# The first mixture's combine: row normalisation by ScalarE with a scale and a bias from GpSimd, in place of VectorE

## The reference, cut to what matters

```python
def _layernorm(x, axis=-1, eps=1e-05):
    m = jnp.mean(x, axis=axis, keepdims=True)
    v = jnp.var(x, axis=axis, keepdims=True)
    return (x - m) / jnp.sqrt(v + eps)

# end of layer 1: two experts for each row, weighted, and one shared expert
x = _layernorm(x + moe(x))            # moe: combine(expert_out) + 0.1 * shared
# start of layer 2
qkv = x @ W_qkv + b_qkv               # 16 heads of 8, alibi bias, softmax, values
```

## Time and profile before

| what | value |
|---|---|
| time, three runs | 1142.61, 1149.12, 1151.37 us; median 1149.12 |
| the profiled execution | 1147.93 us, span 1146.2 us |
| mean granted clock of TensorE | 0.925 |
| TensorE busy (matmuls) | 987.9 us, 86% |
| VectorE busy | 780.8 us, 68% |
| ScalarE busy | 660.6 us, 58% |
| GpSimd busy | 352.7 us, 31% |

### The profile page before, as it was taken

How to read it: one execution, slowest core, us unless ns; L and a number is a source line. 1 busy time by engine, 2 the same in 40 slices (tenths; PEclk the granted TensorE clock), 3 DMA queues, 4 the chain that set the end, 5 groups by cost and what they waited for, 6 DMA issues and landing times.

```text
span 1146.2 us, 18859 instructions
## 1 busy us (share of the span) xinstructions
PE 987.9 (86%) x6456; PEld 500.3 (44%) x6517; DVE 780.8 (68%) x1663; ACT 660.6 (58%) x1282; POOL 352.7 (31%) x541
## 2 busy tenths in 40 slices
PE   5599889999988799366999999898899998988992
PEld 2267634544445588332333333476322222224661
DVE  5976686768742411489788887246888888855875
ACT  4664646566554355052667767575277766685451
POOL 7636510111442335420000000231111221645764
PEclk9799879999999899766999999989599999899997
DMA  5930224333621220333333210002234432311332
GB/s 142 171 73 1 93 102 140 129 119 106 174 79 31 65 64 17 89 94 107 100 122 123 80 65 31 2 1 93 99 112 146 132 99 77 110 29 46 98 102 84
DMA packets 98375, 101.70 MB, mean 89 GB/s; under 512 B 13354, under 2 KB 80571, under 8 KB 98199
## 3 DMA queue, kind: packets, MB, share of 16 engines
q1 hardware_dynamic: 86169, 89.28, 26.6%
q0 software_dynamic: 6432, 8.18, 2.5%
q10 hardware_dynamic: 5680, 3.04, 1.0%
HBM read 66.60 MB, written 38.09 MB: 91 GB/s over the span
## 4 chain that ended last, share of the span: by engine, by line
PE 66%; DVE 18%; issue 5%; ACT 5%; POOL 4%; DMA 2%; SPq 0%; another core or an unknown queue 0%; ACTq 0%; POOLq 0%; DVEq 0%
PE PS L894 13%; PE PS L878 13%; PE PS L851 8%; DVE negm L1696 5%; PE PS L705 5%; PE PS L700 5%; PE PS L1063 3%; PE PS L1073 3%; PE PS L1193 3%; PE PS L881 3%; PE PS L854 2%; PE PS L902 2%; ACT arena L1323 2%; PE PS L1208 2%; DVE X L1551 1%
## 5 line engine op out<-in xcount | busy, mean ns | idle before, releaser
L1323 ACT ACTIVATE arena<-PS 128x512 f32<-128x512 f32 (+3 forms) x768 | 362.5, 548 | 187.9 <-PE PS L881 121.1
L1696 DVE TENSOR_REDUCE negm<-PS 128x2 f32<-128x1024 f32 (+3 forms) x384 | 404.7, 1087 | 89.2 <-PE PS L851 44.5
L878 PE MATMUL PS<-arena 128*128 128x512 bf16 (+3 forms) x707 | 219.8, 363 | 8.4 <-ACT arena L1323 5.1
L894 PE MATMUL PS<-arena,VPAD 128*32 128x512 f32 (+3 forms) x1536 | 188.1, 561 | 0.1
L851 PE MATMUL PS<-arena 32*128 32x512 bf16 (+3 forms) x768 | 144.3, 374 | 29.5 <-DVE negm L1696 25.9
L851 PEld LDWEIGHTS PS<-arena 32*128 32x128 bf16 x768 | 36.4, 91 | 213.4 <-DVE negm L1696 106.9
L878 PEld LDWEIGHTS PS<-arena 128*128 128x128 bf16 x768 | 69.7, 98 | 120.3 <-issue 57.1
L2533 POOL CAST nmp<-negm 128x16 bf16<-128x16 f32 x48 | 9.4, 196 | 360.7 <-DVE negm L1696 241.1
L700 PE MATMUL PS<-arena,W 128*128 128x512 f32 x144 | 84.1, 719 | 12.4 <-ACT arena L1241 9.9
L705 PEld LDWEIGHTS PS<-W,arena 128*128 128x128 f32 x640 | 80.0, 204 | 14.0 <-issue 7.1
L705 PE MATMUL PS<-W,arena 128*128 128x128 f32 x640 | 81.6, 288 | 3.0 <-DVE arena L1640 2.7
(11 more groups left out here) (335 smaller groups left out, 1538.1 us busy)
## 6 DMA issues: line engine op xcount, KB each, us to landing
arena<-score_q SPq DMA_DIRECT2D x48, 288.0 KB
arena<-score_k SPq DMA_DIRECT2D x48, 288.0 KB
arena<-max_parts SPq DMA_DIRECT2D x48, 256.0 KB
max_parts<-arena SPq DMA_DIRECT2D x36, 256.0 KB, 2.9
score_k<-arena SPq DMA_DIRECT2D x36, 128.0 KB
score_q<-arena SPq DMA_DIRECT2D x12, 384.0 KB
arena<-rows_y SPq DMA_DIRECT2D x16, 256.0 KB, 3.9
arena<-slots SPq DMA_DIRECT2D x46, 65.0 KB, 1.9
```

The source lines that it names most:

```text
L878: mm = pe.matmul(PS[:, b, q0:S], OK[s][:, r, kt * P:(kt + 1) * P], OQ[s][:, r, q0:S], start=True, stop=True)
L894: mm = pe.matmul(PS[32 * r:32 * r + 32, 7, q0:S], VP[:, u, kt, r, :], PB[:, kt % 2, r, q0:S], start=(kt == 0), stop=True, skip_group_check ...
L1323: act.activation(PB[:, kt % 2, r, q0:S], PS[:, 4 + use % 3, q0:S], ACT.Exp, scale=slope(u % G, r) if o["slope"] else 1.0).then_inc(exped, 1)
L1696: vec.tensor_reduce(negm[:, u % 2, 2 * rp:2 * rp + 2, qt], PS[:, 2 * (use % 2):2 * (use % 2) + 2, 0:nk], AX.X, ALU.max, negate=True).then_ ...
```

## The change

The step `ln` leaves VectorE and becomes a step of ScalarE: four `activation` instructions with function Identity, the scale `rs` and the bias `nb` = -mean * rs. GpSimd computes `nb` in two further instructions behind the power. TensorE's transposes wait for ScalarE in place of VectorE. The orders of ScalarE and VectorE are rewritten; those of TensorE and GpSimd stay. ScalarE now goes ln 0, xT 0, q 0, k 0 (with the zeros), ln 1, ln 3, xT 1, q 1, k 1 (with the zeros), xT 3, q 3, k 3, ln 2, xT 2, q 2, k 2. VectorE goes tot 0, tot 1, tot 3, split 0, tot 2, split 1, values 0, values 1, and from there on as before. What is computed stays the same.

```diff
-    "cb.a cb.tot", NORM_V.format("cb"), PREP_V.format("p2"),
+    "cb.a cb.tot cb.bn cb.mv", PREP_V.format("p2"),
...
-    "p1.xT p1.q p1.k o1.xT r1.xT", numbered("sh.h", 4), EXPERTS_A, "p2.xT p2.q p2.k",
+    "p1.xT p1.q p1.k o1.xT r1.xT", numbered("sh.h", 4), EXPERTS_A, "cb.ln p2.xT p2.q p2.k",
...
-COMBINE_SCALAR, COMBINE_SCALAR_TURNS = words("xT q k"), "000111333222"
-COMBINE_VECTOR, COMBINE_VECTOR_TURNS = words("tot ln split values"), "001103321201RR3RRRRRRRR32RRR2R"
+COMBINE_SCALAR, COMBINE_SCALAR_TURNS = words("ln xT q k"), "0000131113332222"
+COMBINE_VECTOR, COMBINE_VECTOR_TURNS = words("tot split values"), "01302101RR3RRRRRRRR32RRR2R"
...
                     if step == "tr":
-                        turned_input(c, "p2", "cb.ln")
+                        pe.wait_ge(*A.at(c, "cb.ln"))
+                        turn(c, lanes[c].A, lanes[c].X, "p2.tr")
...
                 for step, c in taken(COMBINE_SCALAR, COMBINE_SCALAR_TURNS):
-                    if step == "xT":
+                    if step == "ln":
+                        L = lanes[c]
+                        act.wait_ge(*PO.at(c, "cb.nb"))
+                        act.wait_ge(*V.at(c, "cb.tot"))
+                        for j in range(CT):
+                            t = act.activation(L.X[:, j, :], L.tot[:, j, :], ACT.Identity, scale=L.rs[:, j:j + 1], bias=L.nb[:, j:j + 1])
+                        t.then_inc(*A.did(c, "cb.ln"))
+                    elif step == "xT":
...
-                    elif step == "ln":
-                        normalised(c, L.tot, L.X, "cb")
...
+                    L = lanes[c]
                     norm(c, "cb")
+                    pool.tensor_scalar(L.nb[:], L.mv[:, :, 0], -1.0, 0.0, ALU.mult, ALU.add).then_inc(*PO.did(c, "cb.nm"))
+                    pool.wait_ge(*PO.at(c, "cb.nm"))
+                    pool.tensor_tensor(L.nb[:], L.nb[:], L.rs[:], ALU.mult).then_inc(*PO.did(c, "cb.nb"))
```

More of the change, by code:

```diff
@@ L115 @@
     "m.va m.rs m.va2 m.rs2 m.lva m.lrs t.va t.rt t.rs t.s2 t.s1 t.va2 t.rt2 t.rs2 t.lva t.lrs o1.lva o1.lrs",
-    "x0.id x1.id cb.lva cb.lrs o2.xb o2.lva o2.lrs ch.xb ch.lva ch.lrs o3.xb r3.id r3.lva r3.lrs r3.nm r3.nb o3.lva o3.lrs r3.sh e.lva e.lrs"]))
+    "x0.id x1.id cb.lva cb.lrs cb.nm cb.nb o2.xb o2.lva o2.lrs ch.xb ch.lva ch.lrs o3.xb r3.id r3.lva r3.lrs r3.nm r3.nb o3.lva o3.lrs r3.sh e.lva e.lrs"]))
 TENSOR_STEPS = words(" ".join([
```

## The result

The changed kernel takes 1152.62 us, the median of 20 runs (1147.48 to 1157.07), against 1146.24 for the kernel before in 20 runs (1142.02 to 1151.99). The ratio is 1.0049 with a 95% interval of 1.0034 to 1.0065, so the change costs 3.9 to 7.5 us, 5.6 by the ratio. The forecast was 7.5 us more than before and 1156.0 us in all; both kernels lie within the 1% of each other that the prediction expected. The profiled execution took 1155.99 us with a span of 1154.0, against 1147.93 and 1146.2.

A forecast was written before the change was run, and what follows sets the result against it. VectorE's chain and ScalarE's with TensorE arrive together at the first maxima; after the change the latter is later. The sum 1.0 + 0.5 + 3.1 + 2.8 + 0.1 = 7.5 us more gave 1156.0 us, range 1150 to 1162.

The forecast's parts named there:

- Step 1: Chunk 0 ahead of its transposes: two added GpSimd instructions and the slower norm on ScalarE, together +1.0 us.
- Step 2: Chunk 0's roots on GpSimd: held up by VectorE's two-input instructions of tot 1, +0.5 us, between 0 and 1.3.
- Step 3: Chunk 1's copy on ScalarE: ln 1 and ln 3 now stand ahead of it, +3.1 us, 4.6 late in all.
- Step 4: Chunk 2: ln 2 queued behind k 3 on ScalarE makes its transposes 7.4 us late, 2.8 beyond the chain's 4.6.
- Step 5: VectorE's first maxima: VectorE idles until TensorE's chunk 2 transposes and first pair are over; start 7.5 us late with semaphore.
- Step 6: Ramp behind the first maxima: VectorE's order takes just as long, so the first scores come 7.5 us late.
- bounds: TensorE's clock around the first maxima: low behind its idle time +1.6 us; high in the first scores -2.3.
- (a): Rival for the ramp: VectorE is the bound and the time falls by 8.7 us, to 1139; chance 0.03.
- (b): Rival: another chain behind the ramp hides the delay and the kernel stays at 1148 to 1150 us; chance 0.12.
- (c): Rival: TensorE's low clock makes the ramp longer, 9.9 us and some loss in first attention units, 1160 to 1163; chance 0.15.

The follow-up runs named there:

- ln3_in_wait: Changed kernel with ScalarE's ln 3 alone moved from ahead of chunk 1's copy to behind it; one run, no time claimed, first maxima 36.82 us into the stage.
- order: Changed kernel with ScalarE's order alone rewritten, each norm but the first in a wait for a chunk's projections; ratio to before 0.9975.
- ln2_in_wait: Changed kernel with ScalarE's ln 2 alone moved from behind k 3 to behind chunk 3's copy; one run, no time claimed, first maxima at 33.28 us.
- ln2_vector: Changed kernel with chunk 2's norm alone given back to VectorE, behind split 1; ratio to before 0.9995.
- before_again: Kernel before, unchanged, profiled a second time on a slower chip, where its median is 1166.12 us; first maxima 31.41 us into the stage.
- before_late_zeros: Kernel before with ScalarE's second zeros moved from behind k 1 to behind k 2; ratio to before 1.0008.
- order_late_zeros: Changed kernel with ScalarE's order rewritten as in order, and the second zeros moved behind k 2; 1142.08 us, ratio to before 0.9958.

## Why the prediction was right

**Step 1** was right: copy of chunk 0 1.00 us late, forecast 1.0.

**Step 2** was wrong, by its 0.5 us: the four GpSimd instructions took the 1.8 us that they take alone. The row of chunk 2 was a row of long instructions, and I scaled it down instead of asking how much short ones do it at all. The Trainium skill's rule (GPSIMD Engine Reference, Key points: contention with instructions of two SBUF inputs) holds for the long instruction, 0.54 us for 0.20; for the short ones it shows on GpSimd's side in two profiles of eight only, with 0.16 us. Without the 0.5 the copies would have been forecast at 20.7 and 29.8, where they are (20.71, 29.70).

**Step 3** had the size right (3.1 forecast, 3.08 measured over chunk 0's) and the division wrong, as ln3_in_wait showed: ln 3 was almost free (0.24 us), because ln 1 keeps TensorE and ScalarE waiting for the same time. The prediction's own numbers held this (copy possible at 504.0, ScalarE free at 504.1) and I read them as "the transposes don't make it later" instead of as "the second norm doesn't either".

**Step 4** had the mechanism right, and order, ln2_in_wait and ln2_vector confirm it, but chunk 2's transposes came 5.5 us late, not 7.4. Of the 1.9, 0.6 was there at the copy of chunk 3 (step 2's 0.5 in the main), and 1.1 is the time from the copy of chunk 3 to ln 2, 4.42 us where the profile of before had 5.52 up to the last copy: I took one execution's slow projections (3.68 us) for a constant. About 0.1 is left over.

**Step 5** was right: first maxima released by TensorE, after 6.43 us of idle time (7 forecast); 5.86 us late in place of 7.5. Of this 5.53 is the start of chunk 2's transposes and 0.33 the time from there to the anchor, 1.77 us for 1.44, mainly since the transposes took 1.11 us at a granted clock of 0.50 where the prediction's sum has 0.66.

**Step 6** said that the ramp takes just as long. It took 24.10 us in place of 22.73, since VectorE waited 1.26 us for the maxima's matmuls behind chunk 2's slow projections, which I had kept under "bounds" only (+1.6). It is not all due to the change: before_again has 1.01 of this wait too, and in the second pair of profiles the ramp differs by 0.3 us only (24.11 against 23.84). The first scores gave back 0.9 (from the end of values 2 to the first evacuated output 22.65 us against 23.57). Together: 5.86 + 1.37 - 0.92 = 6.3 us in the stage; what follows differs by -0.2, what stands ahead by +1.7, and these are the 7.8 us between the spans of the two profiles. The 5.6 us of the ratio and the 6.3 and 6.6 of the two pairs of profiles agree.

**The rivals.** (a) was excluded by the right argument, and before_late_zeros and order_late_zeros show under which condition it does decide: when ScalarE's chain is shortened too. In order, where the norms fill ScalarE's waits, the relief of VectorE is already worth 1.2 to 1.5 us at the anchor. (b) didn't happen: nothing behind the ramp hid the delay. (c) came true in a small part, the longer ramp: 1.4 us in the first pair of profiles, 0.3 in the second. The range of 1150 to 1162 held and the mechanism is the one that was forecast. The size, 7.5 us, was too large: 5.6 us by the ratio, mainly step 2's 0.5 and the 1.1 in step 4. The figure of 1156.0 was 3.4 us too high also because it leaned on 1149.12 from three runs, a median 2.9 us above that of twenty.

## What to carry to other kernels

An engine's busy share doesn't say that moving its work away helps: ask which chains arrive at the same point, and work each one out to that point after the move. A step that moves to another engine takes a place in that engine's queue, and the place costs more than the step: here a norm of 1.65 us behind another chunk's work made the next stage 4.3 us later, clock included (3.5 where the projections ahead of it took the same time), while the same norm in a wait that was there anyway cost the next stage nothing. When two chains end together, try both edits in one kernel, since one of them alone can look worthless.

## What the runs showed of the hardware

- A GpSimd instruction on 4 columns beside VectorE instructions with two SBUF inputs of 128 columns each took as long as alone in six profiles of eight (0.20 and 1.05 us), VectorE's group then 1.23 or 1.24 us for 1.14; in two profiles one took 0.34 us for 0.18, and VectorE's group 1.18. Beside one of 512 columns it lasted until this ended (0.54 us for 0.20), and so beside one of 1024 (1.07 for 0.19).
- A GpSimd memset of 128x4096 floats (3.51 us) delayed VectorE's cast out of SBUF (0.69 us alone; 1.09 and 2.30 beside it, ending 0.55 and 0.56 us after the memset), and not the two-input subtractions beside it (1.23 and 1.22, as alone).
- TensorE's granted clock was at different levels at the same step of the same program: 0.54 and 1.00 in chunk 3's projections (3.68 and 1.98 us), worth 1.7 us on one step. Chunk 2's projections took 3.62 us at 0.50 in both profiles of the changed kernel, behind a pause of 2.9 us, and 1.88 at 1.00 in the four kernels without a pause at this place (order, order_late_zeros, ln2_vector, ln2_in_wait). The pause doesn't decide it alone: behind 3.34 us in before_late_zeros they took 2.35 (0.80), behind 1.91 in before_again 3.57 (0.52). What decides within one program isn't settled by these runs.
